# Order of the rows in the im2col tiles of a 3x3 convolution: tap first, or channel first

## The reference, cut to what matters

```python
xn = layernorm(x, ln1_scale, ln1_bias)
hidden = jnp.einsum('nhwc,co->nhwo', xn, w_hidden)            # 16 -> 192 channels
qkv = lax.conv_general_dilated(hidden, w_qkv, window_strides=(1, 1), padding='SAME',
                               dimension_numbers=('NHWC', 'HWIO', 'NHWC'))   # 3x3, 192 -> 192
q, k, v = jnp.split(qkv, 3, axis=-1)
qp, kp = x_to_patch(q, HEADS, PATCH), x_to_patch(k, HEADS, PATCH)            # 8x8 patches
out = jnp.fft.irfft2(jnp.fft.rfft2(qp) * jnp.fft.rfft2(kp), s=(PATCH, PATCH))
out = layernorm(patch_to_x(out), ln2_scale, ln2_bias)
return jnp.einsum('nhwc,co->nhwo', v * out, w_out) + x
```

## Time and profile before

| | |
|---|---|
| median of three runs | 286.76 us |
| the profiled execution | 287.55 us, of which the span is 285.8 us |
| TensorE matmul busy | 259.6 us, 91% of the span |
| VectorE busy | 164.4 us, 58% |
| ScalarE busy | 144.2 us, 50% |
| GpSimd busy | 75.1 us, 26% |
| mean granted TensorE clock | 0.97 of full speed |
| DMA, queue of SP and ACT | 20.11 MB, 44.7% of 16 engines' span |

### The profile page before, as it was taken

The page is one execution under the profiler, slowest core; times in us unless marked ns, Lnnn a source line. Parts: engine busy times, 40 slices in busy tenths (PEclk is TensorE's granted clock), DMA queues, the critical chain, the costliest instruction groups (busy, mean ns, idle before and its releaser), DMA issues.

```text
span 285.8 us, 6002 instructions
## 1 busy us (share of the span) xinstructions
PE 259.6 (91%) x2264; PEld 183.2 (64%) x2264; DVE 164.4 (58%) x374; ACT 144.2 (50%) x359; POOL 75.1 (26%) x150
## 2 busy tenths in 40 slices
PE   6798999989999993557999999999999999999974
PEld 2467444856466561345887796887877878778643
DVE  3984022564289772403557766756667747576575
ACT  2283646136468550020577565656655656655640
POOL 2809000011030000001345434243342424334310
PEclk9989999999999999695999999999999999999999
DMA  6900000000000369999994899989980000100000
GB/s 256 242 2 14 9 2 1 16 2 0 3 0 0 95 127 131 146 178 138 125 156 135 129 120 118 179 113 116 121 173 1 18 5 0 22 0 3 18 21 18
DMA packets 15468, 21.12 MB, mean 74 GB/s; under 512 B 1882, under 2 KB 10858, under 8 KB 15338
## 3 DMA queue, kind: packets, MB, share of 16 engines
q1 hardware_dynamic: 15120, 20.11, 44.7%
q10 hardware_dynamic: 320, 0.64, 0.7%
HBM read 16.57 MB, written 4.02 MB: 72 GB/s over the span
## 4 chain that ended last, share of the span: by engine, by line
PE 75%; DVE 8%; DMA 7%; SPq 5%; ACT 3%; issue 1%; DVEq 0%; ACTq 0%
PE bank L1092 12%; PE bank L1118 10%; PE bank L1099 7%; PE bank L952 6%; PE bank L1069 5%; PE bank L1014 5%; DMA arena<-parts 5%; PE bank L1130 5%; PE bank L1108 4%; SPq L391 3%; PE bank L981 2%; PE bank L1076 2%; PE bank L1093 2%; PE bank L907 2%; PE bank L968 2%; PE bank L927 2%
## 5 line engine op out<-in xcount | busy, mean ns | idle before, releaser
L1092 PE MATMUL bank<-wc,tile 128*128 128x128 f32 x256 | 49.2, 315 | 12.1 <-DVE tile L796 12.1
L1092 PEld LDWEIGHTS bank<-wc,tile 128*128 128x128 f32 x256 | 41.0, 202 | 20.2 <-issue 13.1
L484 POOL TENSOR_TENSOR pr<-tp 128x120 f32<-128x120 f32 x32 | 14.9, 465 | 135.8 <-DVE tp L827 135.8
L827 DVE TENSOR_TENSOR tp<-bank,kh 128x256 f32<-128x256 f32 x64 | 24.2, 419 | 42.9 <-ACT kh L631 42.9
L796 DVE COPY tile<-arena 128x256 bf16<-128x256 bf16 (+1 forms) x128 | 32.3, 314 | 18.2 <-DMA arena<-parts 17.9
L616 ACT COPY qk<-bank 128x512 f32<-128x512 f32 x32 | 18.7, 585 | 43.9 <-PE bank L1093 43.9
L1118 PE MATMUL bank<-km,qk 128*128 128x128 f32 x256 | 34.8, 280 | 0.0
L1118 PEld LDWEIGHTS bank<-km,qk 128*128 128x128 f32 x256 | 31.9, 196 | 0.9 <-ACT qk L616 0.9
L1093 PE MATMUL bank<-wc,tile 128*128 128x128 bf16 x128 | 29.0, 226 | 0.0
L1099 PE MATMUL bank<-tile,wc 128*64 128x256 f32 (+1 forms) x192 | 25.5, 374 | 0.0
L477 POOL TENSOR_TENSOR zp<-spec 128x256 f32<-128x256 f32 x30 | 22.4, 748 | 0.0
(11 more groups left out here) (129 smaller groups left out, 449.3 us busy)
## 6 DMA issues: line engine op xcount, KB each, us to landing
arena<-padded SPq DMA_DIRECT2D x24, 263.0 KB, 11.9
arena<-parts SPq DMA_DIRECT2D x6, 394.5 KB, 19.9
arena<-padded SPq DMA_DIRECT2D x16, 131.0 KB, 8.4
parts<-tr SPq DMA_DIRECT2D x12, 115.5 KB
wq<-w_qkv SPq DMA_DIRECT2D x1, 1296.0 KB, 12.6
padded<-tr SPq DMA_DIRECT2D x2, 528.0 KB, 11.2
xt<-x SPq DMA_DIRECT2D x2, 512.0 KB, 5.4
out<-xt SPq DMA_DIRECT2D x8, 128.0 KB, 1.9
```

What stands on the lines that cost most here:

```text
L827: o = dve.tensor_tensor(tp[:, m % 2, e].rearrange("p a r s -> p a (r s)"), bank[3][:, 0:256].rearrange("p (a n) -> p a n", a=4), kh[:, m % ...
L1092: mm(bank[n % 2][:, P * t:P * t + P], tile[:, n % 2, t, :], wc[:, 0:2 * CH], start=True, stop=False)
```

## The change

The 128 rows of the contraction get another order. Before, row 16t + c of `ui` holds tap t of channel c, and each tap's load writes 16 adjacent partitions. After, it is row 8c + t: the load of tap t writes partitions t, t + 8, ... t + 120. The same holds for the eight products of parts in `ui9`; since a 48-partition piece can't be written so, `load_last` issues eight DMAs of 16 partitions (66 KB each for half an image, 131 KB for a whole one) in place of three, and the semaphore counts go up to match (`PART_LOADS` from 3 to 8). The weights get the same order of rows. Bytes, lengths of runs, the gathers and all matmuls keep their shapes; a sum over the rows is the same in another order.

```diff
-PAD_STORES, PART_STORES, PART_LOADS = 3, 6, 3
+PAD_STORES, PART_STORES, PART_LOADS = 3, 6, 8
...
-                sp_.dma_start(wc[C * t:C * t + C, :], wfold[32 * j:32 * j + C, HID * e:HID * e + HID]).then_inc(wc_ld, 16)
+                sp_.dma_start(wc[t:P:FULL, :], wfold[32 * j:32 * j + C, HID * e:HID * e + HID]).then_inc(wc_ld, 16)
...
-                sp_.dma_start(wc9[C * r:C * r + C, :], w9s[:, part, :]).then_inc(wc_ld, 16)
+                sp_.dma_start(wc9[r:P:FULL, :], w9s[:, part, :]).then_inc(wc_ld, 16)
...
-                    dst = ui[C * t:C * t + C, 1 - b % 2].rearrange("p x t y -> p x (t y)")
+                    dst = ui[t:P:FULL, 1 - b % 2].rearrange("p x t y -> p x (t y)")
...
-                for row, n in ((0, 3 * C), (3 * C, 3 * C), (6 * C, 2 * C)):
-                    dst = ui9[row:row + n, 1 - b % 2].rearrange("p x t y -> p x (t y)")
-                    sp_.dma_start(dst[:, :, at:at + w], rows[0:n, :, 2 + at:2 + at + w]).then_inc(done, 16)
+                for r, (part, _) in enumerate(SPLIT):
+                    dst = ui9[r:P:FULL, 1 - b % 2].rearrange("p x t y -> p x (t y)")
+                    sp_.dma_start(dst[:, :, at:at + w], rows[C * part:C * part + C, :, 2 + at:2 + at + w]).then_inc(done, 16)
```

## The result

The changed kernel takes 283.05 us (median of four runs, 280.38 to 283.97) against 286.87 for the kernel before (four runs as well; the 286.76 above is of three): 0.985 of its time, 95% interval 0.982 to 0.989. That is faster by 3.8 us (1.5%), a third of the 11.8 us that the forecast of 275.0 stood for, and it lies above the range of 271.5 to 282.5. The profiled execution took 283.62 us with a span of 281.8, 4.0 less than before.

The account below looks back on a forecast made before the run. Loads were taken to bound the kernel in one gap ended by half B: gather(2) 9.35 us earlier plus 2.6 us of clock, 11.95 in total, from 286.76 to 274.8, stated as 275.0 us; range 271.5 to 282.5.

Parts of the forecast that it names:

- What bounds the kernel: Before the loop's steady part: loads bound the kernel in one gap, ended by image 0's half B; the later loop moves unchanged.
- Destination of the taps: Tap loads: spread partitions raise the rate from 125 to 215 GB/s; half A's taps take 5.0 us in place of 8.4.
- Eight pieces in place of three: SP's queue, bfloat16 loads: 0.47 us an issue, 3.8 us in place of 1.46, 2.3 us more for each half.
- rival (a): SP's queue: at 0.63 us per DMA issue becomes the bound, 6.2 us gained, clock falls again, 280.6 us; chance 0.24.
- The two limits: Half B's landing before gather(2): about 120.0 by data and 119.7 by issue, nearly meeting; gather(2) at 120.5.
- The clock: TensorE's step n = 2: idle stretches of about 3 us leave the clock at 2.4 GHz, 2.6 us more gained.
- n = 0 and 1: TensorE's first two loop steps: some 4.7 us at full clock in place of 8, done by 118.3, before gather(2).
- (c): Tap loads: the slow rate comes from the source, so no change, 286.8 us; chance 0.07.
- (d): Loads: any DMA of 16 partitions is slow, so the pieces fall to 125 GB/s, 291.8 us; chance 0.10.
- (b): TensorE goes from n = 1 to n = 2 without a gap, the loads fast enough: 272.1 us; chance 0.05.
- The margin of image 1: Before gather(8): image 1 lands by 138.5 and is wanted at 143.1, a margin of 4.6 us.
- The serial reading: Bfloat16 loads: five more DMAs at a fixed 2 us one after another, 10 us for each half; rejected by the prediction.

Follow-up runs that it names:

- taps_only: The changed kernel with only the taps at a step of 8 partitions, the bfloat16 tile back to three adjacent loads: 277.3 us, 0.968 of before.
- after_warm: The changed kernel with six warming matmuls in place of one ahead of the loop and six more ahead of n = 2: 280.64 us.
- taps_step2: The kernel before with pairs of taps interleaved at a step of 2 in 32 partitions, `wc` likewise: 276.47 us, 0.965 of before.
- adj_pieces: The kernel before with the bfloat16 tile loaded by eight DMAs of 16 adjacent partitions in place of three: 287.36 us, 1.004 of before.
- pieces_only: The changed kernel with the taps back on adjacent partitions, only the bfloat16 tile in eight pieces with a step of 8: 284.69 us, 0.993 of before.
- after_two_queues: The changed kernel with image 0's sixteen bfloat16 pieces issued from ScalarE's queue in place of SP's: 279.23 us, 0.974 of before.

## Why the prediction was wrong, point by point

**What bounds the kernel.** Right for the kernel before: one gap, ended by half B, and a loop behind it that moves as a block. From gather(8) to the end the spans have 130.7 us in the kernel before, the changed one, `taps_only` and `after_warm`.

**Destination of the taps.** Right in sign, cause and size. Forecast 215 GB/s, measured 206 to 212 in the changed kernel (held down by the issue), 209 for image 1 in `taps_only` (not held down) and 221 with two queues, taps and pieces together. The rate of the pieces, which I had at 215 too, was 202 to 207 where they were not bound by the issue. That the cause is the destination's layout is shown, by `taps_only` and `taps_step2` for the taps and by `adj_pieces` against `pieces_only` for the pieces. The ports that the prediction puts behind it were not seen as such; the rates fit them.

**Eight pieces in place of three.** This is the step that failed, the price of an issue. I took 0.47 us for an issue from the first eight taps of the earlier trace rows and carried it over to all 32 of A and B, though the destination had changed its form; I had the 0.63 of the earlier trace rows as the upper bound and put it into rival (a) with a chance of 0.24. Measured: 0.64 for each. 32 x 0.17 = 5.4 us, and one issue of 1.17, 0.5 more: B's last piece leaves SP at 123.7 in place of 117.9, and gather(2) starts at 125.5 in place of 120.5. The landing behind the last issue was right (2.33 us, forecast 2.3).

**The two limits.** I wrote that data (120.0) and issue (119.7) nearly meet and went on with a sum as if either error were small. Where two limits meet, a mistake in either goes to the end nearly in full: the 5.8 us by which B's last piece left SP late became 5.0 at the gather, since gather(2) stood at 120.5 in the sum, 0.8 behind the issue's 119.7. The limit by data was too early as well. With the pieces' issue out of the way gather(2) came at 121.84 (`taps_only`) and 122.67 (two queues), with the engines' share above 1 for most of the ten us before. So of the 5.0 us the issue of the pieces accounts for 3.7, which `taps_only` got back; the last 1.3 would have stayed by that kernel's figures.

**The clock.** Its size was right, 2.6 us forecast, 2.4 between the changed kernel and `after_warm`. That the changed kernel would get it was wrong. TensorE's idle stretches were 5.1 us (110.4 to 115.5) and 3.7 (122.6 to 126.3), not 3, since the loads were late; and the reading "it fell after 5.2 idle us" was no safe distance: in the changed kernel it fell at about 126.0, after 3.4 us of idleness (0.74 is the mean of a window that began at 1.00 and ended at 0.50):

```profile
125.50:126.50 1.00, 0.19 (x1) 0.19 (x2) 1.00 (x5) 0.00 (x0) 0.00 (x0) 0.74 0.36 112
```

The error in one term thus took the other with it: 5.0 + 2.6 = 7.6 of the 11.95 didn't come, which leaves 4.35; the span has 4.0. That SP's issue set gather(2) is shown by the chain, by `taps_only` and by `after_two_queues`, that the 2.6 are the clock's by `after_warm`. A small term was short too: n = 0 and 1 take 5.3 us at full clock (115.58 to 120.88 in `after_warm`), not 4.7; it wasn't on the path.

**Why rival (a) was still too low.** It had the mechanism and nearly the price, 280.6. But it left A's taps at 0.47 (out at 106.6; they were out at 107.7), and it knew nothing of the one issue of 1.17 us in B's taps: they were out at 118.6 in place of 116.7, B's pieces at 123.7 in place of 121.7, and gather(2) started at 125.5 in place of 123.6. The range ended at 282.5 and the median is 283.05. The changed kernel's four runs differ by 3.6 us, and their mean clock with them: 0.987 in the run of 280.38, 0.976 in those of 283.62 and 283.97. By my estimate a step of 5.9 us at 0.50 lowers the mean over a span of 281.8 by 0.010, so the three figures fit a clock's term that is paid in some runs and not in others. Only one of the runs has a trace, so this isn't shown; seventeen later runs of the kernel before differ by 3.2 us too.

**The rivals that fell.** (c), the source, and (d), any DMA of 16 partitions, fell by the taps' own rate and by `adj_pieces` against `pieces_only`. (b), no gap before n = 2, fell by VectorE's wait of 8.0 us. The margin of image 1 held: gather(8) waits for nothing.

**The rule against small transfers.** The serial reading that the prediction rejected, 10 us for each half, was rightly rejected: the pieces cost 3.5 (5.10 against 1.62 us of SP). The advice of the Trainium skill, page "DMA: Bandwidth & Descriptors", section "Rules for kernel authors", to join small transfers holds here all the same, for SP's time and not for the landing's. It speaks of transfers under 64 KB, where the prediction has "at 64 KB"; the pieces have 66.

## What to carry to other kernels

When a load gets faster, work out who feeds it. The time of one issue times the number of issues is a second limit beside bytes over rate; a DMA share that falls to 0.5 while the wait stays was its sign here. Take the price of an issue from a row with the same form of access; with a step between the partitions it was 0.64 us here and not 0.47. And split a change into its parts. Here the layout of the large tile gave 9 us, that of the small one, once the large one was fast, took more than half of it back, and the first alone (277.3, or 276.5 with a step of 2) beats both kernels.

## What the runs showed of the hardware that I had not expected

An issue of a load from DRAM to 16 partitions costs SP 0.47 us with adjacent partitions and 0.64 with a step of 2 or of 8. The 0.64 are the same for 66, 131 and 263 KB (5.08 us for the eight taps of image 1 in `taps_only`). ScalarE's queue took a little more, 0.68 (10.85 for 16). Single issues are longer for no reason that the traces show: 1.17 us in the changed kernel, and in `after_warm` eight that took 5.73 in place of 5.10. The small weight loads, from SBUF to SBUF, cost 0.63 both with adjacent partitions and with a step of 8 (5.01 us for eight in both kernels), so the step isn't the only thing that makes an issue dear; what does was not tried.

The granted clock fell to 0.5 when TensorE had been idle for 5.2 us in the kernel before and for 3.4 in the changed one, and in `taps_only` it fell at about 115, when TensorE, idle for 3.7 us until then, had been at work again for one microsecond (from 113.98).
